# Attention: queries and keys projected for two batches at once, with stack waits, loads and last pieces placed anew

## The chip, the core and the metric

One core of a Trainium2 chip runs the whole program in one launch. The metric is the device time of that core in microseconds. TensorE (PE) multiplies matrices into PSUM; ScalarE (ACT), VectorE (DVE) and GpSimd (POOL) work on the results; SyncE (SP) issues most DMAs. Each engine works through its own instructions in order and waits on semaphores where the program says so.

## The reference, cut to what matters

The reference runs attention, an FFN, a second attention-like block and a last FFN over x of shape (4, 256, 256). The change touches the first attention alone and three loads near it:

```
q, k, v = x @ Wq.T, x @ Wk.T, x @ Wv.T        # 16 heads; q, k: 128 plain + 64 rotary, v: 128
scores  = q_nope k_nope^T / sqrt(128) + rope(q) rope(k)^T / sqrt(64)
out     = softmax(scores) v @ Wo.T            # per batch of 256 tokens
```

Later the first FFN needs W2 turned by a Walsh-Hadamard transform, and the sum of x and the attention's output, layer-normalised.

## The kernel before, in words

All products are made from a high and a low part of each operand, three matmuls for one (hi*hi, hi*lo, lo*hi; helper `three`, lines 312 to 314). Attention has 16 slots: 4 groups of 4 heads times 4 batches. A slot s (k is its place in the unrolled code, s = k in the first two slots) does the attention of 4 heads of one batch, in 4 steps j = 0 to 3, one head each. The order is written out by hand, the same on each engine (`emit`): step j multiplies the scores of head j, turns the probabilities of head j-1, and multiplies probabilities and values of head j-2. Between these stand pieces for later slots: step 0 and 1 project queries and keys of the next slot (pieces 2 to 5; each is q and k of one head pair's half, 2 x 256 columns of one bank), step 2 the rotary parts of the slot after next (pieces 0 and 1), step 3 its values (pieces 6 and 7) and the output product of the slot before. Each piece lands in one of the three PSUM banks PJ; ScalarE copies the high part out of the bank (L599), VectorE subtracts for the low part (L723), and a count in `part_split` tells that the bank is free and the piece is there.

The rotary part goes a long way. VectorE multiplies the bank by the tables (L718, `rope_prod`), POOL adds the halves (`rotate`, L851 and L852), ScalarE copies the high part into rot_h (L596), POOL makes rot_l (L860). SP writes both to scratch memory in DRAM (`spill`, L216: eight DMAs for queries and keys) and reads them back stacked, so that one matmul takes both halves (`fill`: Q2 at L228, K2 and K3 at L233). rot_h and rot_l have one buffer: the next rotary copy waits for the landing of the spill before. SP's list for a slot (`emit` in the sync block) is: in the second slot of a group five loads of raw weights for the next group (L276), in the third slot the other five; then the spill for slot s+2; then its fill. Ahead of the first slot SP has the first fill, then xres (1 MB, L266), had (L267) and W2 (1 MB, L297).

ScalarE and POOL split the next group's weights in the third slot of a group: ScalarE copies two pieces per step, POOL subtracts (`split_piece`, L866), pieces 0 to 3 ahead of the two rotations, 4 and 5 behind them. The rotary projection for the first batch of the next group (step 2 of the third slot) waits until pieces 0 and 1 are split (`w_split`, line 353).

Two users of the late loads matter. POOL, between its work for slots 1 and 2, does half of the additions of the Hadamard transform (L901):

```
pool.wait_ge(w2_in, 32)     # had and W2 have landed
add_tiles(0, 12)
```

and VectorE, in step 1 of slot 2, adds the first output product to xres and waits for its landing (`accumulate`, L753, `res_in`). At the start TensorE warms up with 22 matmuls (L528).

In the last two slots the heads' products take turns between the banks O and PJ2, and slot 15 has the first pieces of the next layer's preparation (`tail`).

Of the kernel before, what the change touches and what calls it, by code (L numbers as in the profile page):

```python
# [39 lines left out]
def attention(nc, keep, x_tok, x_T, w_att, w_ffn0, w2_raw, rope, ident_d, had_d):  # L40
# [13 lines left out]
    with ExitStack() as ctx:  # L54
# [46 lines left out]
        BANK = [1, 2, 0, 1, 2, 0, 0, 1]  # L101
# [70 lines left out]
        ORDER = [([2], [3]), ([4], [5]), ([], []), ([6], [7])]  # L172
        ROPE_STEP = 2
# [3 lines left out]
        TAIL = [(0, 1), (2,), (3,), (4,)]  # L177

# [7 lines left out]
        def rope_bank(k, p):  # L186

            if k < 2:
                return keep["X"] if p else O
            return PJ[BANK[p]]  # L190

# [4 lines left out]
        def bank_of(k, p):  # L196

            if k == 0 and p == 5:
                return PT[:, :, :].rearrange("p t n -> p (t n)")
            return PJ[BANK[p]]  # L200

# [6 lines left out]
        def _(sp):  # L208
# [98 lines left out]
        def _(pe):  # L307
# [32 lines left out]

            def rope_piece(s, k, p):
# [8 lines left out]
                if p == 0:  # L350
                    pe.wait_ge(x_split, b + 1)
                    if b == 0:
                        pe.wait_ge(w_split, GP * (s // 4 if isinstance(s, int) else group[0]) + 2)
                if k == 1:
                    pe.wait_ge(rope_prod, p + 1)
                elif k:
                    pe.wait_ge(part_split, 6 * (s - 1) + 2 + p)
                project(rope_bank(k, p), p, slice(b * S, b * S + S)).then_inc(rope_ready, 1)

            def bank_free(s, k, p):  # L360

                if p == 2 and k:
                    pe.wait_ge(part_split, 6 * s - 1)
                if p == 3 and k:
                    pe.wait_ge(part_split, 6 * s)
                if p == 4 and k == 1:
                    pe.wait_ge(part_split, 3)
                if p == 4 and k > 1:
                    pe.wait_ge(rope_prod, 2 * s + 2)
                if p == 5 and k:  # L370
                    pe.wait_ge(part_split, 6 * s + 1)
                if p == 6:
                    pe.wait_ge(part_split, 6 * s + 4 if k else 1)
                if p == 7:
                    if k in (0, 15):
                        pe.wait_ge(part_split, 6 * s + 2)
                    else:
                        pe.wait_ge(rope_prod, 2 * s + 3)

            def piece(s, k, p):  # L380

                b = k % 4
                out = bank_of(k, p)
                bank_free(s, k, p)
                if b == 0 and p % 2 == 0:

                    pe.wait_ge(w_split, GP * (s // 4 if isinstance(s, int) else group[0]) + 2 + p)
                if p < 6:
                    last = project(out, p, slice(b * S, b * S + S))
                else:  # L390
                    rows = slice(b * S + (p - 6) * P, b * S + (p - 5) * P)
                    last = three(out[:, :], [(xTh[:, t, rows], xTl[:, t, rows]) for t in range(KT)],
                                 [(WBh[:, 6 + t, :], WBl[:, 6 + t, :]) for t in range(KT)])
                last.then_inc(piece_ready, 1)

            def scores(s, k, j):
                u, par, bank = 4 * s + j, k % 2, SC[j % 2]
                if j == 0 and k:
                    pe.wait_ge(stack_q[par], 8 * (s + par))
                    pe.wait_ge(stack_k[par], 32 * (s + par))  # L400
                if j == 0 and not k:
                    pe.wait_ge(rope_lo, 2)
                pe.wait_ge(part_split, 6 * s + j + 1)
                if k > 0 or j >= 2:
                    pe.wait_ge(exp_ready, u - 1)
                for t in range(TT):
                    q, keys = slice(t * P, (t + 1) * P), slice(S, 2 * S)
                    out = bank[:, t, :]
                    both = t > 0 and not k
                    pe.matmul(out, QKh[:, par, j, q], QKh[:, par, j, keys], start=not both, stop=False,  # L410
                              skip_group_check=both)
                    pe.matmul(out, QKh[:, par, j, q], QKl[:, par, j, keys], start=False, stop=False,
                              skip_group_check=both)
                    pe.matmul(out, QKl[:, par, j, q], QKh[:, par, j, keys], start=False, stop=False,
                              skip_group_check=both)
                    if k:
# [45 lines left out]
            def output(s, k, first):  # L462

                if k % 4 == 0:
                    pe.wait_ge(w_split, GP * ((s // 4 if isinstance(s, int) else group[0]) + 1))
# [34 lines left out]
            def emit(s, k):  # L500
                for j in range(HG):
                    u = 4 * s + j
                    scores(s, k, j)
                    if j == ROPE_STEP and k < 14:
                        rope_piece(s + 2, k + 2, 0)
                    if k < 15:
                        for p in ORDER[j][0]:
                            piece(s + 1, k + 1, p)
                    if k > 0 or j >= 1:
                        turn_probs(u - 1, (j - 1) % 4, first=(k == 0 and j == 1))  # L510
                    if j == ROPE_STEP and k < 14:
                        rope_piece(s + 2, k + 2, 1)
                    if k < 15:
                        for p in ORDER[j][1]:
                            piece(s + 1, k + 1, p)
# [15 lines left out]
            for p in range(2, 8):  # L531
                piece(0, 0, p)
# [42 lines left out]
        def part_dst(k, p, hi):  # L575
            if p < 6:
                return (QKh if hi else QKl)[:, k % 2, p - 2, :]
            return (Vh if hi else Vl)[:, k % 2, p - 6, :]
# [10 lines left out]
        def _(act):  # L589
            def part(s, k, p):  # L590
                if p < 2:

                    act.wait_ge(rope_sum, 4 * s + 2 * p + 2)
                    if k > 1:
                        act.wait_ge(spill_k if p else spill_q, 64 * (s - 1))
                    act.activation(rot_dst(k, p, True), rope_f[:, 2 + p, :], ACT.Copy).then_inc(rope_hi, 1)  # L596
                else:
                    act.wait_ge(piece_ready, 6 * s + p - 1)
                    act.activation(part_dst(k, p, True), bank_of(k, p)[:, :], ACT.Copy).then_inc(part_hi, 1)  # L599
# [44 lines left out]
            def emit(s, k, g):  # L644
                for j in range(HG):
# [5 lines left out]
                    if k < 15:  # L651
                        for p in ORDER[j][0]:
                            part(s + 1, k + 1, p)
                    if j == ROPE_STEP + 1 and k < 14:
                        part(s + 2, k + 2, 0)
# [3 lines left out]
                    if k < 15:  # L659
                        for p in ORDER[j][1]:  # L660
                            part(s + 1, k + 1, p)
                    if j == ROPE_STEP + 1 and k < 14:
                        part(s + 2, k + 2, 1)
# [5 lines left out]
                    if k % 4 == 2:  # L669
                        for i in REPLACED[j]:  # L670
                            if i < 2:
                                weight_piece(i, g + 1, (rope_ready, 2 * (s + 1) + 2))
                            else:
                                weight_piece(i, g + 1, (piece_ready, 6 * (s + 1) + i - i % 2))
# [6 lines left out]
            for what, i in START_ACT:  # L681
# [6 lines left out]
                elif what == "r":  # L688
                    part(1, 1, i)
                else:  # L690
                    part(0, 0, i)
# [15 lines left out]
        def _(dve):  # L707
            def part(s, k, p):
                if p < 2:
                    dve.wait_ge(rope_ready, 2 * s + p + 1)  # L710
                    if k > 0 or p:
                        dve.wait_ge(rope_sum, 4 * s + 2 * p)
                    if k == 0:
                        dve.wait_ge(tab_in[p], 16)
                    bank = rope_bank(k, p)[:, :].rearrange("p (c n) -> p c n", c=2)
                    for f in range(2):
                        table = tables[:, p, f:f + 1, :].broadcast_to([P, 2, S])
                        last = dve.tensor_tensor(rope_f[:, f, :].rearrange("p (c n) -> p c n", c=2), bank, table,  # L718
                                                 ALU.mult)
                    last.then_inc(rope_prod, 1)  # L720
                else:
                    dve.wait_ge(part_hi, 6 * s + p - 1)
                    dve.tensor_tensor(part_dst(k, p, False), bank_of(k, p)[:, :],  # L723
                                      part_dst(k, p, True).bitcast(F32), ALU.subtract).then_inc(part_split, 1)
# [51 lines left out]
            def emit(s, k):  # L776
                for j in range(HG):
# [3 lines left out]
                    if j == ROPE_STEP and k < 14:  # L781
                        part(s + 2, k + 2, 0)
                    if k < 15:
                        for p in ORDER[j][0]:
                            part(s + 1, k + 1, p)
# [11 lines left out]
                    if j == ROPE_STEP and k < 14:  # L797
                        part(s + 2, k + 2, 1)
                    if k < 15:
                        for p in ORDER[j][1]:  # L800
# [1424 lines left out]
```

## Time and profile before

| | us |
|---|---|
| median of three runs (670.73 to 671.31) | 671.05 |
| the profiled execution's own time | 671.69 |
| its span, first to last instruction | 669.9 |
| TensorE busy | 656.0 (98%) |
| VectorE busy | 438.9 (66%) |
| ScalarE busy | 410.5 (61%) |
| POOL busy | 245.9 (37%) |
| mean granted TensorE clock | 0.997 |

The profile is of one execution. TensorE's matmuls overlap in it: one of 256 columns lasts 0.28 us, and the next starts 0.12 us after it. What counts for the time is from start to start. A slot's first scores stand at 21.7, 46.7, 71.3, 95.1 and 119.4 us, later slots follow at steps of 23.7.

### The profile page before, as it was taken

The page shows a single profiled execution, that of the slowest core. Times are in us where ns is not written, and L with a number is a line of the kernel's source. Part 1 is how long each engine was busy: PE and PEld are TensorE (multiplying, and loading weights), DVE is VectorE, ACT ScalarE, POOL GpSimd, SP SyncE. Part 2 cuts the span into 40 slices and gives each one's busy share as a digit, 9 for nine tenths or more (in the row PEclk, how much of TensorE's full clock was granted, in tenths as well). Part 3 has the DMA queues.
Part 4 walks back from the last instruction along what each step waited for, and adds up shares of the span by engine and source line. Part 5 has one row for each costly group of instructions (what it writes and reads, how often), then busy time and mean ns, then how long its engine had stood idle before and what let it go on. Part 6 is the DMA issues. An engine that isn't in the chain of part 4 may idle for free. (4 is left out here: it accounts for less than half of the span.)

```text
span 669.9 us, 15243 instructions
## 1 busy us (share of the span) xinstructions
PE 656.0 (98%) x5297; PEld 630.9 (94%) x5297; DVE 438.9 (66%) x952; ACT 410.5 (61%) x1085; POOL 245.9 (37%) x279
## 2 busy tenths in 40 slices
PE   9999999999999999999999999999999999999995
PEld 8989999999999999999999899999996799999995
DVE  6566557557666755765665577556559986556877
ACT  5556667666776666866577774334689964333553
POOL 3731863134353133632328454212361462222011
PEclk9999999999999999999999999999999999999998
DMA  7174655436543435544363404100166200000000
GB/s 254 39 226 139 202 170 145 135 100 174 163 133 111 126 123 170 163 137 118 96 186 120 111 1 151 32 0 0 41 202 246 76 1 1 1 1 0 1 33 31
DMA packets 38172, 69.74 MB, mean 104 GB/s; under 512 B 3440, under 2 KB 22640, under 8 KB 37872
## 3 DMA queue, kind: packets, MB, share of 16 engines
q1 hardware_dynamic: 37696, 68.38, 33.7%
q10 hardware_dynamic: 432, 0.79, 0.4%
q8 instruction: 26, 0.43, 0.3%
q14 instruction: 18, 0.15, 0.1%
HBM read 52.18 MB, written 16.97 MB: 103 GB/s over the span
## 5 line engine op out<-in xcount | busy, mean ns | idle before, releaser
L312 PE MATMUL PJ<-xTh,WBh 128*128 128x256 f32 x364 | 106.8, 293 | 0.1
L314 PE MATMUL PJ<-xTh,WBl 128*128 128x256 f32 x364 | 103.0, 283 | 0.0
L313 PE MATMUL PJ<-xTl,WBh 128*128 128x256 f32 x364 | 102.8, 282 | 0.0
L851 POOL TENSOR_TENSOR stage<-stage 128x256 f32<-128x256 f32 x32 | 24.4, 764 | 162.4 <-DVE stage L718 162.4
L611 ACT ACTIVATE probs<-probs,rinv 128x256 f32<-128x256 f32 x128 | 58.4, 508 | 26.3 <-DVE rinv L734 26.3
L312 PEld LDWEIGHTS PJ<-xTh,WBh 128*128 128x128 f32 x364 | 69.6, 191 | 0.9 <-DVE Vl L723 0.3
L313 PEld LDWEIGHTS PJ<-xTl,WBh 128*128 128x128 f32 x364 | 69.6, 191 | 0.0
L314 PEld LDWEIGHTS PJ<-xTh,WBl 128*128 128x128 f32 x364 | 69.4, 191 | 0.0
L723 DVE TENSOR_TENSOR QKl<-PJ,QKh 128x512 fp32r<-128x512 f32 x63 | 43.4, 689 | 37.2 <-ACT QKh L599 37.0
L866 POOL TENSOR_TENSOR WBl<-raw,WBh 128x512 fp32r<-128x512 f32 x32 | 40.8, 1294 | 30.7 <-ACT WBh L628 30.7
L1091 POOL TENSOR_SCALAR vare<-mv 128x2 f32<-128x2 f32 x13 | 2.9, 223 | 132.1 <-DVE mv L1084 132.1
L604 ACT ACTIVATE probs<-TB,nmax 128x256 f32<-128x256 f32 x64 | 29.8, 471 | 32.7 <-DVE nmax L730 31.2
L604 ACT ACTIVATE probs<-SC,nmax 128x256 f32<-128x256 f32 x64 | 29.8, 471 | 32.0 <-DVE nmax L730 32.0
L738 DVE TENSOR_TENSOR PTl<-PT,PTh 128x512 fp32r<-128x512 f32 x64 | 43.4, 679 | 5.5 <-ACT PTh L617 5.3
L728 DVE TENSOR_REDUCE rmax<-TB 128x2 f32<-128x512 f32 x32 | 22.1, 691 | 37.2 <-PE TB L418 33.9
L1360 DVE TENSOR_TENSOR QKl<-gb,QKh 128x256 fp32r<-128x256 f32 x96 | 42.7, 445 | 0.3 <-ACT QKh L1309 0.3
L860 POOL TENSOR_TENSOR rot_l<-stage,rot_h 128x512 fp32r<-128x512 f32 x30 | 38.7, 1293 | 7.7 <-ACT rot_h L596 7.7
L1309 ACT ACTIVATE QKh<-gb 128x256 fp32r<-128x256 f32 x96 | 39.3, 410 | 2.2 <-DVE gb L1356 1.2
L1304 ACT ACTIVATE ga<-UG 128x256 f32<-128x256 f32 x32 | 12.3, 385 | 44.8 <-PE UG L1235 44.8
L440 PE MATMUL PT<-ident,probs 128*128 128x128 f32 x256 | 38.4, 272 | 0.7 <-ACT probs L611 0.5
L617 ACT ACTIVATE PTh<-PT 128x512 fp32r<-128x512 f32 x64 | 38.7, 604 | 0.5 <-PE PT L440 0.5
L743 DVE TENSOR_TENSOR OTl<-O,OTh 128x256 fp32r<-128x256 f32 x60 | 25.0, 417 | 21.2 <-ACT OTh L621 21.0
(340 smaller groups left out, 2516.1 us busy)
## 6 DMA issues: line engine op xcount, KB each, us to landing
K<-scr_k SPq DMA_DIRECT2D x60, 256.0 KB, 4.4
raw<-in_w_att SPq DMA_DIRECT2D x37, 256.0 KB, 4.8
Q<-scr_q SPq DMA_DIRECT2D x15, 512.0 KB, 7.3
stage<-scr_m SPq DMA_DIRECT2D x6, 768.0 KB, 4.0
scr_q<-rot_h SPq DMA_DIRECT2D x30, 128.0 KB
scr_q<-rot_l SPq DMA_DIRECT2D x30, 128.0 KB
scr_k<-rot_h SPq DMA_DIRECT2D x30, 128.0 KB
scr_k<-rot_l SPq DMA_DIRECT2D x30, 128.0 KB
```

The lines of the kernel that those rows point to most:

```text
L312: pe.matmul(out, ah, bh, start=(i == 0), stop=False)
L313: pe.matmul(out, ah, bl, start=False, stop=False)
L314: last = pe.matmul(out, al, bh, start=False, stop=(i == n - 1))
L604: last = act.activation(probs[:, j % 2, t, :], SC[j % 2][:, t, :], ACT.Exp, scale=SCALE, bias=nmax[:, j % 2, t:t + 1], accum_out=rsum[:, j ...
L611: last = act.activation(probs[:, j % 2, t, :], probs[:, j % 2, t, :], ACT.Copy, scale=rinv[:, j % 2, t:t + 1])
L617: act.activation(PTh[:, j % 2, :, :], PT[:, :, :], ACT.Copy).then_inc(pT_hi, 1)
L723: dve.tensor_tensor(part_dst(k, p, False), bank_of(k, p)[:, :], part_dst(k, p, True).bitcast(F32), ALU.subtract).then_inc(part_split, 1)
L738: dve.tensor_tensor(PTl[:, j % 2, :, :], PT[:, :, :], PTh[:, j % 2, :, :].bitcast(F32), ALU.subtract).then_inc(pT_split, 1)
L860: pool.tensor_tensor(rot_dst(k, p, False), rope_f[:, 2 + p, :].rearrange("p (c n) -> p c n", c=2), rot_dst(k, p, True).bitcast(F32), ALU.s ...
L866: pool.tensor_tensor(weights(i, False), raw[:, i % RING, :], weights(i, True).bitcast(F32), ALU.subtract).then_inc(w_split, 1)
L1309: act.activation(fh[:, ht, :], gb[:, ht % 2, 0:S], ACT.Copy).then_inc(q["f_hi"], 1)
L1360: dve.tensor_tensor(fl[:, ht, :], gb[:, ht % 2, 0:S], fh[:, ht, :].bitcast(F32), ALU.subtract).then_inc(q["f_lo"], 1)
```

## The change

What it does:

1. Queries and keys without the rotary part are projected for two batches by one matmul of 512 columns, from slot 2 on. A piece is now q or k of one head for two batches. Heads 0 and 1 of a pair of slots are projected in the odd slot before them (steps 1 and 2), heads 2 and 3 in the even slot of the pair (steps 0 and 1). QKh and QKl, two buffers by batch before, hold two heads of two batches in each half. The pieces for slot 1 stay as they were.
2. The rotary projection stays at step 2 in even slots and goes to step 0 in odd slots. The banks of the pieces and the counts they wait for follow from that.
3. In the first scores of a slot the six products without rotary part stand ahead of the waits on the stacks (Q2, K2, K3), and the four products with the stacks behind them.
4. SP's loads of had, W2 and xres, in this order, go from ahead of slot 0 to behind the spill for slot 3, in slot 1's list, ahead of the fill for slot 3.
5. The pieces of values in slot 14 go from step 3 (both) to the second half of step 2 and the first half of step 3.
6. POOL makes its two rotations ahead of weight pieces 8 and 9; its split of the down weights waits for the scores of slot 15 that read QKh last.

```diff
-        ORDER = [([2], [3]), ([4], [5]), ([], []), ([6], [7])]
-        ROPE_STEP = 2
+        ROPE_STEP = (2, 0)
+        def pieces(k, j):
+            if k == 14 and j > 1:
+                return [[], [4]] if j == 2 else [[5], []]
+            if k == 15 or j == ROPE_STEP[k % 2]:
+                return [[], []]
+            first = 2 * (j - 1) if k % 2 or j == 3 else 2 * j
+            return [[first], [first + 1]]
+        def rope_now(k, j):
+            return k < 14 and j == ROPE_STEP[k % 2]
...
-            sp.dma_start(xres[:, :, :], x_tok.rearrange("(t p) d -> p t d", p=P)).then_inc(res_in, 16)
-            sp.dma_start(had, had_d).then_inc(w2_in, 16)
+            def load_late():
+                sp.dma_start(had, had_d).then_inc(w2_in, 16)
+                sp.wait_ge(x_split, B)
+                sp.dma_start(w2t[:, :, :].rearrange("p (a b) d -> p a (b d)", b=2), w2_raw).then_inc(w2_in, 16)
+                sp.dma_start(xres[:, :, :], x_tok.rearrange("(t p) d -> p t d", p=P)).then_inc(res_in, 16)
...
                     spill(s + 2, k + 2, 0)
                     spill(s + 2, k + 2, 1)
+                    if k == 1:
+                        load_late()
                     fill(s + 2, k + 2)
-            sp.wait_ge(x_split, B)
-            sp.dma_start(w2t[:, :, :].rearrange("p (a b) d -> p a (b d)", b=2), w2_raw).then_inc(w2_in, 16)
...
+            def project_two(out, at, col, b):
+                w, toks = slice(col * P, (col + 1) * P), slice(b * S, (b + 2) * S)
+                return three(out[:, :], [(WBh[:, at + t, w], WBl[:, at + t, w]) for t in range(KT)],
+                             [(xTh[:, t, toks], xTl[:, t, toks]) for t in range(KT)])
...
+            def piece(s, k, i):
+                n, out = 6 * (s + 1) + i, bank_of(k, i)
+                if k % 2 == 0:
+                    if i == 5 and k < 14:
+                        pe.wait_ge(rope_prod, 2 * s + 5)
+                    elif i < 5:
+                        pe.wait_ge(part_split, n - (1, 1, 4, 2, 0)[i])
+                    if k % 4 == 0 and k and i == 0:
+                        pe.wait_ge(w_split, GP * group_of(s) + 6)
+                    if k == 0 and i < 4:
+                        last = project(out, i + 2, slice(S, 2 * S))
+                    elif i < 4:
+                        last = project_two(out, 4, i, k % 4)
                     else:
+                        last = project_values(out, TT * (k % 4 + 1) + i - 4)
...
             def scores(s, k, j):
-                if j == 0 and k:
-                    pe.wait_ge(stack_q[par], 8 * (s + par))
-                    pe.wait_ge(stack_k[par], 32 * (s + par))
+                apart = not k or j == 0
+                if k < 2:
+                    pe.wait_ge(part_split, 6 * s + j + 1)
+                elif k % 2 == 0:
+                    pe.wait_ge(part_split, 6 * s + (2, 4, 8, 10)[j])
...
+                if apart and k:
+                    pe.wait_ge(stack_q[par], 8 * (s + par))
+                    pe.wait_ge(stack_k[par], 32 * (s + par))
+                    for t in range(TT):
+                        q, out = slice(t * P, (t + 1) * P), bank[:, t, :]
+                        pe.matmul(out, Q2[:, par, j, q], K2[:, par, j, :], start=False, stop=False,
+                                  skip_group_check=t > 0)
+                        last = pe.matmul(out, Q2[:, par, j, q], K3[:, par, j, :], start=False, stop=True,
+                                         skip_group_check=t > 0)
...
             def split_down(q):
                 pool.wait_ge(tail_hi, q + 1)
+                pool.wait_ge(scores_ready, 4 * (SLOTS - 1) + q // 2 + 1)
```

In POOL's part of the program the lines with `w2_in` and `add_tiles` are as before.

## Rows read from the trace of the kernel before

**Rows 1.** The page, part 1: busy us (share of the span) x instructions.

```profile
PE 656.0 (98%) x5297; PEld 630.9 (94%) x5297; DVE 438.9 (66%) x952; ACT 410.5 (61%) x1085; POOL 245.9 (37%) x279
```

**Rows 2.** Busy time by stretch, one slot's length; the columns follow the engines' names.

```profile
114.00:138.00 24.00, 24.00 (x193) 23.43 (x192) 14.96 (x32) 15.08 (x43) 5.42 (x6) 1.00 0.47 127
```

**Rows 3.** Timeline, TensorE: start us, length us, engine, line, operation, tiles.

```profile
45.85 0.28 PE L314 MATMUL O<-PTh,Vl 128*128 128x256 f32 x1
46.70 0.36 PE L410 MATMUL SC<-QKh 128*128 128x256 f32 x1 [0.57 <-issue]
...
70.33 0.28 PE L314 MATMUL O<-PTh,Vl 128*128 128x256 f32 x1
71.33 0.38 PE L410 MATMUL SC<-QKh 128*128 128x256 f32 x1 [0.72 <-DMA K<-scr_k]
```

**Rows 4.** Waits of TensorE, 16 to 370 us: total, times, longest us.

```profile
PE O L312 <- DVE OTl L743: 0.6, 1, 0.6
```

**Rows 5.** Timeline, TensorE, matmuls of 256 and of 512 columns.

```profile
120.59 0.28 PE L312 MATMUL PJ<-xTh,WBh 128*128 128x256 f32 x1
...
121.92 0.28 PE L314 MATMUL PJ<-xTh,WBl 128*128 128x256 f32 x1
...
207.38 0.40 PE L312 MATMUL PJ<-WBh,xTh 128*128 128x512 f32 x1
...
208.54 0.39 PE L314 MATMUL PJ<-WBh,xTl 128*128 128x512 f32 x1
```

**Rows 6.** Timeline of SP's queue in a later slot.

```profile
191.39 1.07 SPq L216 DMA_DIRECT2D scr_q<-rot_l  x2
...
203.84 2.41 SPq L233 DMA_DIRECT2D K<-scr_k  x4
```

**Rows 7.** Timeline of SP's queue, slots 0 to 2.

```profile
41.59 0.59 SPq L266 DMA_DIRECT2D xres<-in_x_tok  x1
42.22 0.75 SPq L267 DMA_DIRECT2D stage<-in_had_d  x1
43.01 0.66 SPq L297 DMA_DIRECT2D w2t<-in_w_raw  x1
...
46.92 4.41 SPq L216 DMA_DIRECT2D scr_q<-rot_l  x2
...
63.89 3.14 SPq L233 DMA_DIRECT2D K<-scr_k  x4
67.13 2.43 SPq L276 DMA_DIRECT2D raw<-in_w_att  x5
69.61 1.17 SPq L216 DMA_DIRECT2D scr_q<-rot_h  x2
...
76.17 2.57 SPq L216 DMA_DIRECT2D scr_k<-rot_l  x2
```

**Rows 8.** DMA issues: line engine operation xcount, KB each, median us to landing.

```profile
raw<-in_wl_d SPq DMA_DIRECT2D x1, 1280.0 KB, 8.3
...
w2t<-in_w_raw SPq DMA_DIRECT2D x1, 1024.0 KB, 10.1
```

**Rows 9.** Timeline of POOL, slot 2.

```profile
70.49 0.72 POOL L901 TENSOR_TENSOR stage<-w2t 128x256 f32<-128x256 f32 x1
...
80.14 2.54 POOL L866 TENSOR_TENSOR WBl<-raw,WBh 128x512 fp32r<-128x512 f32 x2
```

**Rows 10.** Timeline, TensorE, slot 2, first rotary matmul.

```profile
83.08 0.28 PE L312 MATMUL PJ<-xTh,WBh 128*128 128x256 f32 x1
```

**Rows 11.** Timeline of VectorE, slot 2, the accumulate.

```profile
81.58 0.68 DVE L753 TENSOR_TENSOR xres<-X,xres 128x512 f32<-128x512 f32 x1
```

**Rows 12.** Busy time by stretch at the end; PEclk is the granted clock.

```profile
660.00:664.00 4.00, 3.18 (x23) 2.60 (x21) 3.22 (x9) 1.30 (x4) 0.32 (x1) 1.00 0.19 66
...
666.00:668.00 2.00, 0.00 (x0) 0.00 (x0) 0.94 (x4) 0.00 (x0) 0.88 (x3) 0.57 0.20 66
```

**Rows 13.** Timeline, TensorE, the warm-up at the start.

```profile
1.30 5.06 PE L528 MATMUL SC<-rot_h 128*128 128x256 f32 x22 [1.30 <-POOL rot_h L903]
```

More of the change, by code:

```diff
@@ L358, in rope_piece, with project_values @@
                 project(rope_bank(k, p), p, slice(b * S, b * S + S)).then_inc(rope_ready, 1)
[L360 to L371, printed above, removed]
+            def project_values(out, tile):
+                rows = slice(tile * P, (tile + 1) * P)
+                return three(out[:, :], [(xTh[:, t, rows], xTl[:, t, rows]) for t in range(KT)],
+                             [(WBh[:, 6 + t, :], WBl[:, 6 + t, :]) for t in range(KT)])
@@ L380, in piece @@
[L380 to L389, printed above, removed]
-                else:
-                    rows = slice(b * S + (p - 6) * P, b * S + (p - 5) * P)
-                    last = three(out[:, :], [(xTh[:, t, rows], xTl[:, t, rows]) for t in range(KT)],
-                                 [(WBh[:, 6 + t, :], WBl[:, 6 + t, :]) for t in range(KT)])
-                last.then_inc(piece_ready, 1)
+                    pe.wait_ge(part_split, 2)
@@ L396, in scores, with query, key @@
+            def query(part, k, j, rows):
+                if k < 2:
+                    return part[:, k, j, rows]
+                return part[:, j // 2, 2 * (j % 2), (k % 2) * S + rows.start:(k % 2) * S + rows.stop]
+            def key(part, k, j):
+                if k < 2:
+                    return part[:, k, j, S:2 * S]
+                return part[:, j // 2, 2 * (j % 2) + 1, (k % 2) * S:(k % 2 + 1) * S]
             def scores(s, k, j):
                 u, par, bank = 4 * s + j, k % 2, SC[j % 2]
-                if j == 0 and k:
-                    pe.wait_ge(stack_q[par], 8 * (s + par))
-                    pe.wait_ge(stack_k[par], 32 * (s + par))
+                apart = not k or j == 0
@@ L531, in _ @@
             for p in range(2, 8):
-                piece(0, 0, p)
+                first_piece(p)
             for p in range(2):
@@ L650, in emit @@
                     exps(u, j)
[L651 to L655, printed above, removed]
+                    for i in pieces(k, j)[0]:
+                        part(s, k, i)
+                    if j and rope_now(k, j - 1):
+                        rope_part(s + 2, k + 2, 0)
                     if k > 0 or j >= 1:
@@ L658, in emit @@
                     normalise(u, j)
[L659 to L663, printed above, removed]
+                    for i in pieces(k, j)[1]:
+                        part(s, k, i)
+                    if j and rope_now(k, j - 1):
+                        rope_part(s + 2, k + 2, 1)
                     if k > 0 or j >= 2:
@@ L688, in _ @@
                 elif what == "r":
-                    part(1, 1, i)
+                    rope_part(1, 1, i)
+                elif i < 2:
+                    rope_part(0, 0, i)
                 else:
-                    part(0, 0, i)
+                    first_part(i)
             for s in (0, 1):
@@ L707, in _, with rope_part, first_part, part @@
         def _(dve):
[L708 to L724, printed above, removed]
+            def rope_part(s, k, p):
+                dve.wait_ge(rope_ready, 2 * s + p + 1)
+                if k > 0 or p:
+                    dve.wait_ge(rope_sum, 4 * s + 2 * p)
+                if k == 0:
+                    dve.wait_ge(tab_in[p], 16)
+                bank = rope_bank(k, p)[:, :].rearrange("p (c n) -> p c n", c=2)
+                for f in range(2):
+                    table = tables[:, p, f:f + 1, :].broadcast_to([P, 2, S])
+                    last = dve.tensor_tensor(rope_f[:, f, :].rearrange("p (c n) -> p c n", c=2), bank, table,
+                                             ALU.mult)
+                last.then_inc(rope_prod, 1)
+            def first_part(p):
+                dve.wait_ge(part_hi, p - 1)
+                dve.tensor_tensor(first_dst(p, False), first_bank(p)[:, :], first_dst(p, True).bitcast(F32),
+                                  ALU.subtract).then_inc(part_split, 1)
+            def part(s, k, i):
+                dve.wait_ge(part_hi, 6 * (s + 1) + i + 1)
+                dve.tensor_tensor(part_dst(k, i, False), bank_of(k, i)[:, :], part_dst(k, i, True).bitcast(F32),
+                                  ALU.subtract).then_inc(part_split, 1)
             def row_max(u, j):
@@ L780, in emit @@
                         row_max(u, j)
[L781 to L785, printed above, removed]
+                    if rope_now(k, j):
+                        rope_part(s + 2, k + 2, 0)
+                    for i in pieces(k, j)[0]:
+                        part(s, k, i)
                     if j == ACC_STEP and 1 < k < 15:
@@ L796, in emit @@
                         accumulate(13, 13)
[L797 to L800, printed above, removed]
-                            part(s + 1, k + 1, p)
+                    if rope_now(k, j):
+                        rope_part(s + 2, k + 2, 1)
+                    for i in pieces(k, j)[1]:
+                        part(s, k, i)
                     if (k > 0 or j >= 2) and not (k == 14 and j == 1):
@@ L869, in emit @@
             def emit(s, k, g):
-                if k == 5:
-                    for i in (8, 9):
-                        split_piece(GP * g + i, i)
                 if k % 4 == 2:
@@ L879, in emit @@
                         rotate(s + 2, k + 2, p)
+                if k == 5:
+                    for i in (8, 9):
+                        split_piece(GP * g + i, i)
                 if k % 4 == 2:
```

113 lines of the change are left out of this document (71 added, 42 removed).

## The prediction

> **What bounds the kernel now.** I read the page first: TensorE is busy for 98% of the span [rows 1]. Then the engines by stretch: in attention TensorE is busy for all 24.00 of 24 us, VectorE and ScalarE for 15 each, so over a steady stretch only fewer or shorter matmuls shorten it, and anything that makes TensorE stand adds to the time [rows 2]. A slot has 188 matmuls (40 scores, 24 for the rotary part, 48 for queries and keys, 12 for values, 16 transposes, 24 for the heads, 24 for the output); the stretch holds 193 in 24 us, so a slot is some 23.5 us. Third, the waits of TensorE and the timeline around them: between 16 and 370 us it stands only at the first scores of slots 1 and 2 and once in slot 14 [rows 3, 4]. Fourth, the queues of the two slow helpers, SP and POOL, between 40 and 90 us: there the change moves two loads of 1 MB.
>
> **Pairing the projections.** A queries-and-keys piece was 12 matmuls of 256 columns; for two batches it is 12 of 512. The starts of twelve of 256 columns, from 120.59 to 121.92, are 0.12 us apart; six of 512 columns go from 207.38 to 208.54, 0.232 apart [rows 5]. So 24 x 0.12 = 2.88 us become 12 x 0.232 = 2.78 us for a pair. Batches 2 to 15 are paired, 7 pairs x 4 pieces = 28: 28 x 0.1 = 2.7 us less. The columns stay, only the cost per instruction goes. ScalarE and VectorE split as many pieces of 128x512 as before. The row has the same form (512 columns moving) with other operands; if it gains nothing, this term is 0; with the shortest spacing in these rows, 0.23, it is 28 x 12 x 0.01 = 3.4. I take 2.7.
> The Trainium skill (TensorE: Matmul & The Clock Gate, Back-to-back issue gap) gives a fixed cost of about 2.5 ns per warm matmul beyond its columns. Rows 5 show more, some 13 ns beyond the 107 of 256 columns at 2.4 GHz; by the page the pairing would be worth only 336 x 2.5 ns = 0.8 us, 2 us less than my term. I follow the rows.
>
> **Stack waits moved behind six products.** At slot 1 the last start before the wait is 45.85, the next 46.70: 0.85, so 0.73 over the pitch. At slot 2 it is 70.33 to 71.33: 0.88 over [rows 3]. Six matmuls of 0.12 now go ahead, 0.72 us, and cover the first. The second goes too, since the fill of slot 2 comes earlier (below). Together -1.6 (bounds 0 and -1.6). Elsewhere nothing waits there.
>
> **Last pieces redealt.** In slot 14 TensorE waits 0.6 us for VectorE ahead of a head's values [rows 4]. A piece of values (1.39 us) now stands in that gap; but it waits for the split of the piece issued one step before, so it may wait itself. Between +0.5 and -1.1; I take -0.5. The new wait in POOL's down-weight split is for scores that its own input already lies behind: 0.
>
> **Queries and keys in one buffer, other banks, rotary part at step 0 of odd slots.** The first reader of a piece now comes a step of 44 matmuls (5.2 us) later where it was a slot; a copy and a subtraction on two engines that are busy for 15 of 24 us lie between [rows 2]. The rotary copy of an odd slot now comes two steps (10.4 us) earlier, so 13 us after that of the even slot in place of 23.5, and must wait until that one's spill has landed: 12.45 us from the first rot_l issue (191.39) to the key fill that waits for the landing (203.84) [rows 6]. There is about 1 us of slack, and ScalarE isn't full. Cost 0 to 3 us, I take 0.
>
> **The loads: the large term.** SP works in order. Before, xres and W2 were issued at 41.6 and 43.01, and lay in the queue ahead of the spill and fill for slot 2; now they come behind the spill of slot 3, inside the emit of slot 1. Step by step:
> 1. The first rot_l issue for slot 2's rotary part stays at 46.92. The key fill follows 12.45 us later [rows 6], at 59.4, where it was at 63.89 [rows 7]: 4.5 us earlier. Slot 2 finds its keys there.
> 2. Five weight loads (67.13) and the spill for slot 3 (69.61, its last issue ending at 76.17 + 2.57 = 78.74) follow at once, as before; moved up by 4.5 they end at 74.2. The earlier rotary step doesn't help: SP, not the rotary part, is late there.
> 3. had takes 0.75; W2 is issued at about 75.0 and xres after it.
> 4. W2 lands 10.1 us after issue in the row of before, with another load ahead of it; 1280 KB on a quiet queue took 8.3 us, so 1 MB 6.6 us [rows 8]. I take 8.3: 83.3.
> 5. POOL, after the rotary work of emit 1, waits for W2 in line 919 and only then adds 12 tiles. Before, W2 had long landed: adds from 70.49 on, 9.65 us, then the splits of the next group's first two weight pieces, 2.54 us, ending at 82.68 [rows 9]. The first rotary matmul of step 2 of slot 2 (batch 4, so the next group's weights) waits for just these two splits and starts at 83.08 [rows 10]: 0.4 us after them. This cover is now gone.
> 6. After the change: 83.3 + 9.65 + 2.54 + 0.1 = 95.6 for that matmul. Without a wait it would start at 83.08 - 1.6 - 0.2 - 0.2 (four paired pieces each in slots 1 and 2) = 81.1. TensorE stands for 14.5 us.
> Bounds: W2 issued at 72 (spill issued without the backlog) and landing in 6.6 gives 78.6 and 9.8 us; issued at 76.4 and landing in 10.1 gives 86.5 and 17.7 us. Behind the stalled rotary piece on TensorE stand all transposes, values and scores, so nothing runs ahead. VectorE has the same fate earlier: accumulate of slot 2 (81.58 before [rows 11]) waits for xres, which lands after W2. It is late by some 7 us, still ahead of 95.6, and hides in the same stall. POOL's rotate and ScalarE's next weight copy come after the splits too, but in the order in which TensorE then needs them.
> The Trainium skill (DMA: Bandwidth & Descriptors, Queues, rings and completion order) says that the descriptors of a ring are consumed in ring order but that completion is not FIFO per issuing engine. The rows agree with the first half: with 2 MB in the queue the fill waited 4.5 us longer. If W2 needn't wait for the spill's slow writes, it lands at the lower bound of step 4, 1.7 us earlier.
>
> **The clock.** At the end of the kernel, with the last matmul near 663 and TensorE idle from then on, the granted clock is 0.57 in 666 to 668, so it has fallen to 1.2 GHz within it [rows 12]. 14.5 us idle will do the same. At the start 22 matmuls of 256 columns took 5.06 us, 0.23 each in place of 0.12 [rows 13]: if it takes as long to come back, 22 x 0.11 = 2.4 us. Bounds 0 and 2.4; I take 2.4, that being the only row of a rise.
>
> **Sum.** -2.7 - 1.6 - 0.5 + 14.5 + 2.4 = +12.1 us. Against the profiled execution's own 671.69 (span 669.9) that is 683.8; it lies 0.64 above the median of the three runs, 671.05, so the median becomes 683.1. Everything after attention is as before and starts later by the same amount.
>
> **Rivals.**
> A. The loads come in time, and the change gives what it takes out: 671.05 - 4.8 = 666.3. W2 would have to land by 81.1 - 12.3 = 68.8. Against it: SP has the key fill of slot 2, five loads and eight spill issues ahead. Chance 0.09; a cancelling of the two within 0.2% another 0.03.
> B. The queue runs faster: W2 issued near 71 and landed near 77, 8.2 us of stall, 1 us of clock: 675.5. For it: xres and W2 no longer crowd this stretch. Against: the backlog in rows 7 comes from loads and spill themselves, which stay. Chance 0.10.
> C. Not POOL but VectorE decides: W2 lands soon, xres late, and only the accumulate stalls, near 6.5 us with 1 of clock: 673.8. Needs W2 ten microseconds ahead of xres, which is the next in the queue. Chance 0.04.
> D. The forecast, and the rotary copies in odd slots wait for the spill, or POOL's backlog reaches slot 3: 2 to 4 us more, 686. Chance 0.08.
> The forecast itself has 0.66, own range 678 to 687.
>
> **How the numbers follow.** 0.2% (1.3 us) is about what can be told from no change. Slower: 0.66 + 0.10 + 0.04 + 0.08 = 0.88; same 0.03; faster 0.09. The range reaches down into B and up through D: 675 to 688.
>
> **What would show it.** Right: one gap of 10 to 18 us in TensorE in slot 2, ended by POOL's WBl split, with POOL idle before its first add until W2 lands at 80 to 86; a stretch at half clock behind it; SP's W2 issue near 75; 512-column projections 0.232 apart; no wait at the first scores of slots 1 and 2. Wrong: adds that begin before 70, or a steady slot that is longer than before.

## The result, and the profile after

The changed kernel takes 687.0 us (median of six runs, 684.85 to 688.3), the kernel before beside it 671.18: slower by a ratio of 1.0232 (95% interval 1.0212 to 1.0253). The forecast was 683.1, in a range of 675 to 688.

The page of the changed kernel first. TensorE is busy for as long as before with 336 matmuls fewer, but the span has grown from 669.9 to 686.0, so it must stand somewhere. The row PEclk (the granted clock in tenths, for 40 equal slices of the span) says where to look: it dips in slices 6 and 23.

```profile
span 686.0 us, 14564 instructions
PE 656.8 (96%) x4961; PEld 615.7 (90%) x4961; DVE 438.7 (64%) x952; ACT 411.7 (60%) x1085; POOL 245.0 (36%) x279
...
PEclk9999969999999999999999899999999999999999
```

Then the lengths of the slots, from one slot's first scores to the next one's, read off the timelines of both (us):

| slot | before | after | difference |
|---|---|---|---|
| 0 | 24.97 | 24.25 | -0.7 |
| 1 | 24.63 | 23.73 | -0.9 |
| 2 | 23.79 | 39.85 | +16.1 |
| 3 | 24.28 | 23.49 | -0.8 |
| 4 to 13 together | 236.97 | 235.00 | -2.0 |
| 14 | 22.07 | 27.10 | +5.0 |
| 15 | 23.13 | 22.75 | -0.4 |
| behind attention | 268.35 | 268.17 | -0.2 |

Two slots lose 21.1 us, everything else together gains 5.0. What TensorE waited for between 16 and 420 us (engine, line, releaser: total, times, longest) names both losses, and the waits at a slot's first scores [rows 3] are gone from it:

```profile
PE PJ L335 <- POOL WBl L949: 14.4, 1, 14.4
PE PJ L335 <- DVE QKl L806: 2.6, 1, 2.6
PE PT L511 <- ACT probs L689: 0.9, 2, 0.7
```

**Slot 2.** Four timelines of the changed kernel, in the order of the chain: SP's queue (answers to [rows 7]), POOL ([rows 9]), TensorE ([rows 10]), VectorE ([rows 11]).

```profile
59.31 2.42 SPq L251 DMA_DIRECT2D K<-scr_k  x4
61.83 2.43 SPq L299 DMA_DIRECT2D raw<-in_w_att  x5
64.30 1.16 SPq L234 DMA_DIRECT2D scr_q<-rot_h  x2
...
71.63 2.58 SPq L234 DMA_DIRECT2D scr_k<-rot_l  x2
74.25 1.24 SPq L287 DMA_DIRECT2D stage<-in_had_d  x1
75.54 0.43 SPq L289 DMA_DIRECT2D w2t<-in_w_raw  x1
```

```profile
83.60 0.72 POOL L984 TENSOR_TENSOR stage<-w2t 128x256 f32<-128x256 f32 x1 [22.23 <-DMA w2t<-in_w_raw]
...
93.09 4.95 POOL L949 TENSOR_TENSOR WBl<-raw,WBh 128x512 fp32r<-128x512 f32 x4
```

```profile
80.98 0.28 PE L480 MATMUL SC<-K,Q 128*128 128x256 f32 x1
...
95.63 0.58 PE L335 MATMUL PJ<-xTh,WBh 128*128 128x256 f32 x1 [14.37 <-POOL WBl L949]
```

```profile
88.93 0.69 DVE L836 TENSOR_TENSOR xres<-X,xres 128x512 f32<-128x512 f32 x1 [9.59 <-DMA xres<-in_x_tok]
```

Read them from the bottom of the wait upwards. TensorE stands from 80.98 to 95.63, for POOL's second weight split. POOL began those splits at 93.09, straight after its adds; ahead of the adds it had been idle for 22.23 us, for W2, which SP issued at 75.54 and which took 8.0 us to land. VectorE's wait for xres, 9.59 us, begins at 79.34, 1.6 us ahead of TensorE's last start, and is over at 88.93, 6.7 us before TensorE resumes, so it adds nothing to TensorE's. The stretches behind it, with the granted clock as the third figure from the end:

```profile
80.00:84.00 4.00, 1.26 (x11) 1.06 (x9) 0.00 (x0) 0.00 (x0) 0.40 (x1) 1.00 1.04 380
84.00:88.00 4.00, 0.00 (x0) 0.00 (x0) 0.00 (x0) 0.00 (x0) 3.61 (x6) 0.73 1.07 207
88.00:92.00 4.00, 0.00 (x0) 0.00 (x0) 3.03 (x6) 2.27 (x6) 3.61 (x6) 0.50 0.43 115
...
95.60:98.00 2.40, 2.37 (x11) 2.37 (x12) 0.00 (x0) 0.00 (x0) 2.40 (x2) 0.50 0.75 203
98.00:100.00 2.00, 2.00 (x13) 2.00 (x13) 1.30 (x3) 0.55 (x1) 0.05 (x1) 0.62 0.66 199
100.00:102.00 2.00, 2.00 (x19) 2.00 (x19) 0.75 (x2) 1.26 (x5) 1.45 (x2) 1.00 0.25 85
```

The clock fell to 1.2 GHz (0.50) with TensorE idle since 81 us and was still there when it resumed: 11 matmuls in 2.4 us, then 19 in 2.

**Slot 14.** The timeline of TensorE (first fence) and of VectorE (second) in step 2. The first piece of values needs PSUM bank 0, where the last piece of step 1 lies until VectorE has split it; that split comes behind the row maximum of this step's scores. TensorE stands for 2.57 us, and the next matmuls of 512 columns are 0.43 us apart, not 0.23: half clock again (granted clock 0.50 from 384 to 388 us).

```profile
383.52 0.79 PE L335 MATMUL PJ<-WBh,xTh 128*128 128x512 f32 x1 [2.57 <-DVE QKl L806]
384.11 0.63 PE L336 MATMUL PJ<-WBl,xTh 128*128 128x512 f32 x1
384.54 0.63 PE L337 MATMUL PJ<-WBh,xTl 128*128 128x512 f32 x1
```

```profile
381.37 0.68 DVE L811 TENSOR_REDUCE rmax<-SC 128x2 f32<-128x512 f32 x1
382.08 0.79 DVE L813 TENSOR_SCALAR nmax<-rmax 128x2 f32<-128x2 f32 x1
382.79 0.68 DVE L806 TENSOR_TENSOR QKl<-PJ,QKh 128x512 fp32r<-128x512 f32 x1
```

**The pairs.** Timeline of TensorE, six matmuls of a paired piece: 0.232 us apart as in [rows 5], and a steady slot is 23.48 us where it was 23.70.

```profile
162.92 0.40 PE L335 MATMUL PJ<-xTh,WBh 128*128 128x512 f32 x1
...
164.08 0.39 PE L337 MATMUL PJ<-xTh,WBl 128*128 128x512 f32 x1
```

### The profile page after: what moved, and what is told of

It reads as the page before. It is cut to its first block and busy times, and to the rows that moved or that the text cites. A ratio compares the mean times of both kernels' runs of the same rounds, so it can differ in the third digit from the quotient of the medians.

```text
span 686.0 us, 14564 instructions
## 1 busy us (share of the span) xinstructions
PE 656.8 (96%) x4961; PEld 615.7 (90%) x4961; DVE 438.7 (64%) x952; ACT 411.7 (60%) x1085; POOL 245.0 (36%) x279
## 5 line engine op out<-in xcount | busy, mean ns | idle before, releaser
L335 PE MATMUL PJ<-xTh,WBh 128*128 128x256 f32 (+1 forms) x252 | 88.6, 352 | 14.4 <-POOL WBl L949 14.4
L336 PE MATMUL PJ<-xTl,WBh 128*128 128x256 f32 (+1 forms) x252 | 84.2, 334 | 0.0
L337 PE MATMUL PJ<-xTh,WBl 128*128 128x256 f32 (+1 forms) x252 | 84.0, 333 | 0.0
L335 PEld LDWEIGHTS PJ<-xTh,WBh 128*128 128x128 f32 x252 | 48.6, 193 | 17.5 <-POOL WBl L949 14.6
L806 DVE TENSOR_TENSOR QKl<-PJ,QKh 128x512 fp32r<-128x512 f32 x60 | 41.4, 689 | 25.6 <-ACT QKh L677 25.4
L337 PEld LDWEIGHTS PJ<-xTh,WBl 128*128 128x128 f32 x252 | 48.4, 192 | 5.0
L336 PEld LDWEIGHTS PJ<-xTl,WBh 128*128 128x128 f32 x252 | 48.7, 193 | 2.3
L795 DVE TENSOR_TENSOR stage<-PJ,tables 128x512 f32<-128x512 f32 x56 | 36.0, 684 | 8.8 <-PE PJ L337 8.1
```

What stands on the lines that cost most here:

```text
L335: pe.matmul(out, ah, bh, start=(i == 0), stop=False)
L336: pe.matmul(out, ah, bl, start=False, stop=False)
L337: last = pe.matmul(out, al, bh, start=False, stop=(i == n - 1))
L806: dve.tensor_tensor(part_dst(k, i, False), bank_of(k, i)[:, :], part_dst(k, i, True).bitcast(F32), ALU.subtract).then_inc(part_split, 1)
```

## The experiments

Ratios are to the kernel before, run beside each; in brackets the 95% interval.

**The loads alone, on the kernel before.**

```diff
 # before.py: had, W2 and xres from ahead of slot 0's list
                     spill(s + 2, k + 2, 1)
+                    if k == 1:
+                        load_late()      # had, W2, xres
                     fill(s + 2, k + 2)
```

> The kernel before with one edit, its loads of had, W2 and xres moved as the change moves them. Theory (the loads alone make the loss): W2 issued near 76.5, landed near 85, first rotary matmul of step 2 of slot 2 at 97.3 in place of 82.2, 15 us of waiting and 2 at half clock, less 0.9 for the earlier fill of slot 2: 670.4 + 16.3 = 686.7. Rival (only with the shared buffer or the earlier rotary step do the late loads cost that much): under 680.

684.9 us, 1.0206 (1.0191 to 1.0221). TensorE's timeline in slot 2:

```profile
81.55 0.28 PE L422 MATMUL SC<-K,Q 128*128 128x256 f32 x1
95.34 0.58 PE L316 MATMUL PJ<-xTh,WBh 128*128 128x256 f32 x1 [13.51 <-POOL WBl L870]
```

Slot 2 takes 39.62 us. The order of the loads by itself makes the loss; buffer, pairing and rotary step have no part in it. The expectation was 1.8 too high: W2 was issued at 75.26, not 76.5, and landed at 83.17, not 85. Slot 1 takes 23.76 us here, 0.87 less than before, with no other edit: the earlier fill for slot 2 takes away the wait at slot 2's first scores.

**POOL's adds later, the loads as changed.**

```diff
-            pool.wait_ge(w2_in, 32)
-            add_tiles(0, 12)
+            for k in range(2, 6):
+                emit(k, k, k // 4)
+                if k == 3:
+                    pool.wait_ge(w2_in, 32)
+                    add_tiles(0, 12)
```

> The changed kernel with its late loads, but POOL waits for W2 and adds its 12 tiles after its work for slot 3, not ahead of that for slot 2. Theory (W2's wait in POOL decides, and VectorE's wait for xres is hidden behind it): the wait for POOL goes, and what was hidden comes out: the accumulate waits for xres to 88.9 us, the turn of the probabilities in step 2 stands from about 82.5 to 90.7, 8.2 us, and half clock for some of the rest, so slot 2 takes 23.6 + 8.2 + 1.5 = 33.3 and the time is 680.5. Rival (POOL's wait is all of it): slot 2 takes 24 us and the time is 671. Second rival (the queue's traffic holds slot 2 whatever POOL does): slot 2 stays at 38 us or more.

681.31 us, 1.0157 (1.014 to 1.0174); slot 2 takes 33.83. POOL's wait is gone, and TensorE now stands at the turn of the probabilities, 82.44 to 90.26:

```profile
90.26 1.12 PE L511 MATMUL PT<-ident,probs 128*128 128x128 f32 x4 [7.55 <-ACT probs L689]
```

ScalarE's normalising waited for VectorE, and VectorE's longest wait is for xres:

```profile
DVE xres L836 <- DMA xres<-in_x_tok: 8.3, 1, 8.3
```

So two waits lay one over the other; taking away the longer gives back 6 us of 16, not all.

**TensorE kept at work through the wait.**

```diff
+                    if k == 4 and isinstance(s, int):
+                        pe.wait_ge(part_split, 6 * (s - 2) + 8 + p)
+                        for _ in range(118):
+                            pe.matmul(PJ[1][:, 0:S], xTh[:, 0, 0:P], xTh[:, 0, 0:S], start=True, stop=True)
                     if b == 0:
                         pe.wait_ge(w_split, GP * group_of(s) + 2)
```

> The changed kernel, with 118 matmuls of 256 columns, whose result nothing reads, put into TensorE's wait of 14.5 us in slot 2, so that the engine works until just before the weights are split. Theory (slot 2 pays about 2 us for matmuls at 1.2 GHz behind the wait): the granted clock stays at 1.00 there, slot 2 takes 37.7 in place of 39.85, and the time is 685. Rival (the clock costs nothing here, the rest of slot 2 is bound by what POOL and VectorE still owe): 687, slot 2 as long as before.

685.87 us, 1.0212 (1.0188 to 1.0236). Slot 2 takes 37.97 in place of 39.85, and the stretch behind the wait has the full clock and 20 matmuls in 2 us, where the changed kernel has 11 in 2.4:

```profile
96.00:98.00 2.00, 2.00 (x20) 2.00 (x19) 0.79 (x2) 0.45 (x1) 1.82 (x2) 1.00 0.74 206
```

The clock's part of the loss is 1.8 us: from the first rotary matmul of step 2 to the end of the slot it is 12.13 us (95.38 to 107.51) in place of 13.89 (95.63 to 109.52). The remaining 0.1 is a shorter wait. The medians come from different rounds, and their difference (1.1) is within their scatter; the slot is the measure.

**The loads back at the front, the rest of the change kept.**

```diff
-                    if k == 1:
-                        load_late()
+            load_late()      # xres, had, W2, ahead of slot 0's list
```

> The changed kernel with xres, had and W2 issued where they were before, ahead of slot 0's list. Theory (the late loads cost slot 2 16 us: 14.5 of waiting, the rest at half clock): slot 2 falls from 39.85 to about 23.6 us plus a wait of 0.9 for the fill at its first scores, so 687.0 - 16.2 + 0.9 = 671.7. Rival (another part of the change, the shared buffer or the rotary step, is what holds slot 2 and would do so again in a smaller way): slot 2 stays above 27 us and the time above 675.

678.24 us (675.19 to 681.99), 1.0117 (1.0071 to 1.0163). My theory missed by 6.5, though slot 2 is down to 23.50: slot 1 takes 29.43 in place of 23.73. ScalarE's and then TensorE's timeline in slot 1:

```profile
58.24 0.63 ACT L668 ACTIVATE rot_h<-stage 128x512 fp32r<-128x512 f32 x1 [3.05 <-DMA scr_q<-rot_l]
...
63.68 0.63 ACT L668 ACTIVATE rot_h<-stage 128x512 fp32r<-128x512 f32 x1 [3.04 <-DMA scr_k<-rot_l]
```

```profile
65.18 0.45 PE L334 MATMUL O<-PTh,Vh 128*128 128x256 f32 x1 [2.92 <-DVE OTl L825]
```

With 2 MB in the queue ahead of it, the spill for slot 2 lands at 63.6; with the rotary copy two steps earlier, ScalarE waits for it in step 1 and everything else of ScalarE with it. The two edits belong together: the earlier rotary step needs the queue clear in slots 0 and 1. Slot 14 takes 25.89 us here, slots 3, 7 and 11 0.6 to 0.9 more than their neighbours.

**Other banks for the values of slot 14.**

```diff
 def bank_of(k, i):
+    if k == 14 and i > 3:
+        return PJ[5 - i]
```

(and the counts waited for to match)

> The changed kernel, in slot 14 the two pieces of values change banks: the first takes bank 1, free since the second piece of step 0, the other bank 0. Theory (slot 14 is long because the first piece waits 2.7 us for the split of the piece of step 1 in the same bank, and half clock follows): slot 14 falls from 27.1 to about 22, so 687.0 - 5 = 682.0. Rival (the redeal itself, one piece of values in step 2, is what makes it long, by ScalarE's order): slot 14 stays above 25 us, 685 or more.

683.78 us, 1.0205 (1.0188 to 1.0222); slot 14 takes 22.25 in place of 27.10. The bank was the cause. It isn't shorter than the 22.07 of before, so the redeal brings nothing there. The size of the loss varies: with the banks as the change has them slot 14 takes 27.10 and 26.96 us in two profiles (the changed kernel, TensorE kept at work) and 25.84 and 25.89 in two others (POOL's adds later, the loads at the front). In all four TensorE stands 2.6 us for the same split; in the last two the clock is at half for a shorter while behind it. So 3.8 to 5.0 us are lost against the 22.07 of before, and the medians of the changed kernel and this one are 3.2 apart, not 5.0.

**Both.** The two edits above together.

> Both edits, the early loads and the changed banks in slot 14. Theory (the two faults are independent): 671.7 - 5.0 = 666.7, 4.4 us under the kernel before. Rival (the clock or a shared chain ties them): the two gains don't add up, off by more than 1.5 us.

673.5 us, 1.0045 (1.003 to 1.006), against 666.7 expected, with the same fault in slot 1 (28.93). From the loads at the front to both it is 4.7 less. Whether the two gains add up stays open: by the medians they are 8.8 and 3.2 from the changed kernel, and 13.5 together, 1.5 more than their sum, which is just the bound that was set. By the slots each fault is a slot's own: slot 14 is 22.27 here and 22.25 with the banks alone, and slot 1 is long with either set of banks (29.43 and 28.93).

**A mended kernel.** xres behind the fill for slot 2, had and W2 where the change has them, POOL's adds behind slot 3, the exchanged banks.

```diff
                     fill(s + 2, k + 2)
+                    if k == 0:
+                        sp.dma_start(xres[:, :, :], ...).then_inc(res_in, 16)
```

> The changed kernel with three amendments: xres issued behind the fill for slot 2 (in slot 0's list), W2 and had where the change has them but POOL's wait and 12 adds behind its work for slot 3, and the two pieces of values of slot 14 in exchanged banks. Theory (slot 2 was held by W2 in POOL with xres behind it, slot 14 by a bank, and nothing else is wrong): slot 2 takes 23.6, slot 14 22.3, span 665.5, time 667.0, against 670.4 of the kernel before. Rival (xres in the queue between the fill of slot 2 and the weight loads delays the spill and fill of slot 3 or the weights, 2.6 to 4.4 us later, and slot 2 or 3 waits in its place): 669 to 673.

673.79 us, 1.0042 (1.003 to 1.0054): the rival. Slot 2 is at 23.48, slot 3 takes 28.54. ScalarE's waits between 60 and 125 us begin with

```profile
ACT WBh L711 <- DMA raw<-in_w_att: 8.4, 1, 8.4
```

and TensorE's with

```profile
PE PJ L338 <- DVE Vl L811: 2.5, 1, 2.5
```

SP issued that weight load at 86.92, behind W2 (78.35) and the key fill for slot 3 (83.64), and it landed at 95. ScalarE's high copy of the values comes behind that wait, VectorE's split behind the copy, and TensorE stands for the split. The wait had moved to the next engine that owns a place in the same queue.

**The pairs undone** in the mended kernel.

```diff
-                return three(out[:, :], ..., toks of two batches)
+                for c in range(2):
+                    last = three(out[:, c * S:(c + 1) * S], ..., toks of batch b + c)
```

> The mended kernel with each 512-column projection for two batches written as two of 256 columns; the same columns, the same order of pieces. Theory (the pair saves 0.24 - 0.232 us per matmul, 336 of them, as the trace before had it): 2.7 us slower than the mended kernel, a slot 0.2 us longer. Rival by the page's fixed cost of 2.5 ns: 0.8 us slower. Second rival (the shorter slot isn't TensorE's matmuls but the earlier rotary step): no difference.

675.05 us, 1.0059 (1.0043 to 1.0076); a steady slot takes 23.70, not 23.48. That is 0.22 a slot. Slots 1 and 14 have paired pieces too but are as long either way (23.68 and 23.69; 22.27 both), so at most slots 2 to 13 gain, 12 x 0.22 = 2.6, against 2.7 by [rows 5] and the estimate of 0.8 from the 2.5 ns that the Trainium skill gives for isolated matmuls (TensorE: Matmul & The Clock Gate, Back-to-back issue gap). Between the medians only 1.3 are left: the mended kernel waits 0.3 us in slot 7 and 0.6 in slot 11 for a head's split that comes behind the earlier rotary copy, which the longer slots cover.

**The stack waits in front again** in the mended kernel.

```diff
                 apart = not k or j == 0
+                if j == 0 and k:
+                    pe.wait_ge(stack_q[par], ...); pe.wait_ge(stack_k[par], ...)
```

> The mended kernel with the waits on the stacks ahead of the first six products of a slot again. Theory: only slot 1 waits for its fill there, 0.7 us, so 0.7 slower than the mended kernel (slot 0 to 1 24.95 in place of 24.23). Rival (the waits also held later slots): 2 us or more.

672.74 us (671.16 to 677.33), 1.0032 (1.0015 to 1.0048): no slower than the mended kernel, and not told apart from it. Slot 0 is 24.28, not 24.95, since the fill for slot 1 landed in time in this run; at the first scores of slot 3 TensorE waits 1.8 us, but the wait for the split of values behind it is shorter for that, so the two come to about as much as in the mended kernel. The clock then fell to half (0.50 from 98 to 102 us), and slots 2 and 3 together take 1.3 us longer. Inconclusive for the edit's worth: the profiled spans have it 0.9 us longer (671.7 against 670.8), the medians 1.1 shorter.

**W2 later still**, behind the fill for slot 4.

```diff
-                    if k == 1:
-                        load_late()
                     fill(s + 2, k + 2)
+                    if k == 2 and isinstance(s, int):
+                        load_late()
```

> The mended kernel with had and W2 loaded behind the fill for slot 4, in slot 2's list, in place of behind the spill for slot 3; POOL's adds stay behind its work for slot 3. Theory (in the mended kernel slot 3 took 28.5 us because the second half of the next group's weights, issued at 86.9, lay in the queue behind W2 and the key fill, and ScalarE waited 8.4 us for the first of them): that wait falls to the 5.4 us of the kernel before or less, slot 3 takes 23.5 to 24.3, and the time is 673.8 - 4.5 = 669.3, 1.4 under the kernel before. Rival (W2's place doesn't matter, the key fill and the weights alone hold ScalarE that long since slot 2 now begins 1.7 us earlier): slot 3 stays at 28, 673.5.

669.53 us, 0.9982 (0.9968 to 0.9996). Through a slip this kernel and the next load W2 a second time in slot 6, over the sums POOL had made of it, so the first FFN works with other weights; attention isn't touched. Slot 3 is down from 28.54 to 25.72, ScalarE's wait for the weights to 5.6 us. That is still 1.4 us above the 23.5 to 24.3 expected, though the time came out as forecast.

**The last weight load behind the spill** in the third slot of a group.

```diff
-                    for i in range(RING, pieces):
+                    for i in range(RING, pieces if last_group else pieces - 1):
...
                     spill(s + 2, k + 2, 1)
+                    if k % 4 == 2 and not last_group:
+                        ... load(GP - 1)
```

> The kernel with W2 later, and in the third slot of a group the last weight load goes behind the spill in SP's list, not ahead of it. Theory (in slots 3, 7 and 11 ScalarE's copy of the earlier rotary part waits for the landing of the spill before, whose issue SP holds back until POOL has split a weight piece; TensorE then stands 0.2 to 0.8 us for a head's bank): those waits go, 1 us less than the kernel without this edit, 668.3. Rival (the spill's issue waits for the rotary copies themselves, not for the load ahead of it): no difference.

668.91 us, 0.9968 (0.9955 to 0.998). Slots 7 and 11 are both 23.51, as in the kernel without the edit (23.49 and 23.51); slot 3 went from 25.72 to 25.01. The medians differ by 0.6, and the theory's 1 us isn't shown. The profile without the edit has no wait in slots 7 and 11 to take away, so they decide nothing between theory and rival; and slot 3 takes 25.53 in the next kernel, which has the edit too, so 0.7 there is no more than profiles differ by.

**The same with W2 loaded once.**

```diff
-                    if k == 2 and isinstance(s, int):
+                    if isinstance(s, int) and s == 2:
                         load_late()
```

> The kernel with W2 later and the last weight load behind the spill, with had and W2 loaded once, in slot 2's list (the two kernels before it loaded them a second time, in slot 6, over the tiles that POOL had added). Theory: attention as in the kernel with the load behind the spill, its end near 398.2, and everything behind it as in the kernel before, 268.3: span 666.5, time 668.3, 2.4 us under the kernel before. Rival (the second load of W2 made part of what was won): 670 or more.

668.54 us (667.23 to 671.71), 0.9965 (0.9951 to 0.9978): 2.4 under the kernel before and 18 under the change. Its page, where TensorE is back at 98%:

```profile
span 666.6 us, 14450 instructions
PE 651.7 (98%) x4961; PEld 610.4 (92%) x4961; DVE 439.3 (66%) x952; ACT 411.0 (62%) x1085; POOL 245.9 (37%) x279
```

## Why the prediction was right, and where it was off

- The loads: right in the mechanism and close in every link. SP's key fill 59.4 forecast, 59.31 measured; end of the spill 74.2 and 74.21; W2's issue 75.0 and 75.54, its landing 83.3 and 83.5; the held matmul 95.6 and 95.63; the time stood 14.5 and 14.53. The chain could be worked out since most links are rows of before shifted by one number, the 4.5 us by which the key fill came earlier. That the sum agrees to 0.1 us is in part luck: had took 1.24 us in the queue, not 0.75, and against that W2 landed in 8.0 us, not 8.3, and the adds took 9.49, not 9.65. The 8.3 was a choice between bounds of 6.6 and 10.1, not a reading.
- xres hidden under W2: right, VectorE's 9.59 us end before TensorE's 14.5 do, and they cost 7.7 by themselves once W2 was out of the way.
- The clock: 2.4 forecast, 1.8 by the kernel that kept TensorE at work. Taking all 22 warm-up matmuls for the rise was somewhat too many.
- The pairs: 2.7 forecast, 0.22 us in each steady slot measured, at most 2.6 over slots 2 to 13. In slot 1 TensorE waits 0.2 us behind the earlier rotary copy, and nothing is gained.
- The stack waits: -1.6 forecast; slots 0 and 1 are 0.7 and 0.9 shorter. The 0.9 is the moved loads', not this edit's: the loads alone give 0.87 of it. The 0.7 is shown for this pair of traces alone: with the waits in front slot 0 took 24.97, 24.61 and 24.28 us in three kernels (before, the loads alone, the waits in front again), with them behind it took 24.25.
- "Last pieces redealt" failed: -0.5 with bounds of +0.5 and -1.1, measured +5.0 (slot 14). The step saw that the piece waits for the split of the piece before, and took that wait for about as long as the gap it fills. By the sum's own terms it is the one that failed. It left out what VectorE has queued ahead of that split (the turned probabilities, a head, a row maximum that itself waits for this step's scores), and that the clock could fall in such a wait. Both are in the profile: 2.57 us, and 0.43 us between starts. Exchanged banks removed all of it. This is more than the forecast's shortfall (12.1 forecast, 16.1 of span): 5.5 us too little here, 0.6 too much for the clock, and small gains that no term had, 0.6 in slot 3 beyond the pairs, 0.4 in slot 15 and 0.2 behind attention.
- The rotary step, taken as 0 to 3: as good as nothing in the changed kernel (0.2 us in slot 1 and in slot 7), but only because its loads stay out of slots 0 and 1. I had not seen that dependence; it cost the kernel with the loads at the front its expectation.

## What to carry to other kernels

A load has two addresses: the queue it enters and the engine that waits for it. Before moving one, write down for each consumer what stands behind its wait in that engine's program, and shift the trace's own rows along that chain; here that gave the stall to 0.1 us, with three errors of 0.2 to 0.5 that cancelled. When two waits overlap, removing the longer uncovers the other, so both loads need a place of their own; and a piece given an earlier place needs a bank that is free by then, not merely a gap in TensorE.

## What the runs showed of the hardware that was not expected

TensorE's clock fell in slot 14 too: with the transposes' last start at 380.68 and the next matmul at 383.52, matmuls of 512 columns then started 0.43 us apart. The same happened in the kernel with the loads at the front, where it stood from 61.86 to 65.18. But a stop of this length doesn't always do it: in the mended kernel TensorE stood for 2.7 us between the starts at 95.09 and 97.82, and the clock stayed at 1.00:

```profile
96.00:98.00 2.00, 0.18 (x1) 0.18 (x2) 0.76 (x2) 2.00 (x8) 1.35 (x2) 1.00 0.10 40
98.00:100.00 2.00, 1.96 (x16) 1.72 (x16) 1.33 (x2) 2.00 (x7) 1.01 (x2) 1.00 0.15 32
```

In four of the experiments' profiles (both, the pairs undone, W2 later, the last weight load behind the spill) the clock was at half for some us near 520 us too, behind attention, where the program is the same in all of them; the part behind attention took 268.9 to 270.7 us in them, 268.2 to 268.5 in the others. Why is open. Differences of about 1 us between medians may hold some of it, which is why the slots are the measure here.

The moved xres took 12.8 us to land, with W2 ahead of it in the queue, where it had taken 8.9.
